# A GRU and MoE kernel on one core: the bias b_hn is added by a TensorE matmul in the exact steps, from halves made at the end of the preparation

## What is computed

```python
def cell(h, x):
    gi = x @ W_ih + b_ih
    gh = h @ W_hh + b_hh
    i_r, i_z, i_n = jnp.split(gi, 3, axis=-1)
    h_r, h_z, h_n = jnp.split(gh, 3, axis=-1)
    r = jax.nn.sigmoid(i_r + h_r)
    z = jax.nn.sigmoid(i_z + h_z)
    n = jnp.tanh(i_n + r * h_n)
    h_new = (1.0 - z) * n + z * h
```

## Time and profile before

| | us |
|---|---|
| median of three runs | 842.39 (841.79 to 842.82) |
| the profiled execution | 841.37 |
| its span in the trace | 839.6 |
| TensorE busy in the span | 803.8 (96%) |
| VectorE busy | 621.6 (74%) |
| ScalarE busy | 423.0 (50%) |
| GpSimd busy | 180.7 (22%) |

### The profile page before, as it was taken

One profiled execution on the slowest core, in us unless ns is written; L12 is line 12 of the kernel. 1 busy time (PEld: TensorE's weight loads), 2 busy tenths in 40 slices (PEclk: granted clock), 3 DMA queues, 4 the chain that ended last, 5 costly groups with the idle time before them and its releaser, 6 DMA issues.

```text
span 839.6 us, 27893 instructions
## 1 busy us (share of the span) xinstructions
PE 803.8 (96%) x11573; PEld 520.2 (62%) x11574; DVE 621.6 (74%) x2104; ACT 423.0 (50%) x885; POOL 180.7 (22%) x459
## 2 busy tenths in 40 slices
PE   7999999999999999999995799999999999999996
PEld 3446656678999899999994544454444444444442
DVE  6969999868888888888887879776667576855400
ACT  0677676645566556555544538351845184417400
POOL 1002222224333333343331020121012101210011
PEclk9999999999999999999996999999999999999998
DMA  8900000000111010000000952462246324530021
GB/s 333 368 1 3 2 2 2 2 3 7 64 54 42 17 42 5 4 4 4 5 4 14 260 182 101 151 198 53 100 150 176 73 100 150 164 86 1 1 26 26
DMA packets 24281, 62.62 MB, mean 75 GB/s; under 512 B 4384, under 2 KB 4384, under 8 KB 22304
## 3 DMA queue, kind: packets, MB, share of 16 engines
q1 hardware_dynamic: 19312, 51.42, 17.8%
q0 software_dynamic: 3584, 8.42, 5.5%
q10 hardware_dynamic: 1264, 1.08, 0.4%
HBM read 52.49 MB, written 12.62 MB: 78 GB/s over the span
## 4 chain that ended last, share of the span: by engine, by line
PE 80%; DVE 14%; ACT 2%; issue 2%; DMA 1%; POOLq 0%; DVEq 0%
PE ps L454 20%; PE ps L657 20%; PE ps L671 20%; PE ps L446 10%; DVE wa L1212 4%; PE ps L429 3%; DVE wa L1217 3%; DVE halves L1228 2%; ACT wa L767 2%; PE ps L464 2%; PE ps L419 2%; PE ps L591 1%; DVE ocand L1221 1%; PE ps L644 1%; DVE big L1504 1%
## 5 line engine op out<-in xcount | busy, mean ns | idle before, releaser
L454 PE MATMUL ps<-halves,wa 128*128 128x64 f16 x8448 | 287.7, 193 | 5.7 <-DVE halves L1228 2.2
L454 PEld LDWEIGHTS ps<-halves,wa 128*128 128x128 f16 x8448 | 271.0, 98 | 33.1 <-DVE halves L1228 14.2
L671 PE MATMUL ps<-big 128*128 128x512 f16 x768 | 166.9, 379 | 0.0
L657 PE MATMUL ps<-hx,big 128*128 128x512 f16 x768 | 166.9, 379 | 0.0
L767 ACT ACTIVATE wa<-ps,un_gates 128x128 f32<-128x128 f32 x288 | 100.2, 366 | 106.5 <-PE ps L454 100.1
L671 PEld LDWEIGHTS ps<-big 128*128 128x128 f16 x768 | 75.1, 98 | 89.9
L657 PEld LDWEIGHTS ps<-hx,big 128*128 128x128 f16 x768 | 74.9, 98 | 89.9 <-issue 0.2
L772 ACT ACTIVATE wa<-wa,un_gates 128x64 f32<-128x64 f32 x288 | 99.1, 344 | 60.0 <-DVE wa L1217 53.5
L1212 DVE SCALAR_TENSOR_TENSOR wa<-ps,bhn_s,wa 128x64 f32<-128x64 f32 x288 | 80.1, 278 | 52.9 <-ACT wa L767 52.9
L446 PE MATMUL ps<-hx,wb 128*128 128x512 f16 x432 | 106.9, 379 | 1.4 <-issue 1.4
L849 ACT ACTIVATE hx<-ps,un_hid_in 128x512 f32<-128x512 f32 x64 | 43.7, 682 | 109.2 <-PE ps L657 108.0
(11 more groups left out here) (209 smaller groups left out, 707.5 us busy)
## 6 DMA issues: line engine op xcount, KB each, us to landing
wa<-in_w SPq DMA_DIRECT2D x28, 1024.0 KB, 5.1
hs_rows<-big SPq DMA_DIRECT2D x8, 512.0 KB, 6.5
big<-in_w_hh SPq DMA_DIRECT2D x4, 768.0 KB, 19.5
wb<-in_w SPq DMA_DIRECT2D x12, 256.0 KB, 2.5
big<-in_w_ih SPq DMA_DIRECT2D x2, 1024.0 KB, 12.2
hx<-in_x_t SPq DMA_DIRECT2D x2, 1024.0 KB, 16.2
big<-in_w_ih ACTq DMA_DIRECT2D x2, 512.0 KB, 6.5
wa<-in_x_t SPq DMA_DIRECT2D x2, 512.0 KB, 6.1
```

What stands on the lines that cost most here:

```text
L454: mm = pe.matmul(gate_ps[:, j, g, :], whh_parts[:, k, w, (4 * g + j) * P:(4 * g + j + 1) * P], halves[:, src, k, h, :], start=False, stop= ...
L657: mm = pe.matmul(ps[:, m % 2, :], w1p[:, w, k, m * P:(m + 1) * P], tokT[:, t, k, :], start=(k == 0 and n == 0), stop=(k == KD - 1 and n == 2))
L671: mm = pe.matmul(ps[:, 2 + g % 2, :], hid[:, h, k, g * P:(g + 1) * P], w2p[:, w, k, :], start=(k == 0 and n == 0), stop=(k == KH - 1 and n ...
```

## The change

The vector `b_hn` comes in a second time, as a row of 512. Near the start VectorE clears the buffer `carried`, here called `bhn_row`, and ScalarE's queue loads the row into its partitions 0 and 32. At the end of the preparation the new function `split_bhn` finds a power of two as the scale, writes the scaled row in fp16 to `bhn_parts` (partition 0), what fp16 lost to partition 32, and fills `bhn_unit`, 128 x 64 in bf16, with the factor that undoes the scale. All other partitions of `bhn_parts` are zero, so one matmul of `bhn_parts` with `bhn_unit` adds the bias of a tile to all 64 columns. In each exact step `inject(j)` issues that matmul after its two. `reset` becomes a TENSOR_TENSOR in exact steps and stays as it was in rough steps.

```diff
+        bhn_row = carried[:, :, :, :].rearrange("p d k c -> p (d k c)")
+        bhn_parts = sb("bhn_parts", [P, D], F16)
+        bhn_unit = sb("bhn_unit", [P, COLS], BF16)
+        bhn_scales = sb("bhn_scales", [P, 3])
+        ROW_OF = (0, 32)
...
                     pe.matmul(gate_ps[:, j, 0:2, :], diag[:, :], gi_rz[:, c, j, part, :, cols],
                               start=(part == HIGH), stop=False, skip_group_check=True)
+                if LOW in parts:
+                    pe.matmul(gate_ps[:, j, 2, :], bhn_parts[:, j * P:(j + 1) * P], bhn_unit[:, :], start=False,
+                              stop=False, skip_group_check=True)
...
             pe.wait_ge(S["whh_ready"], WHH_PIECES)
+            pe.wait_ge(S["bhn_split"], 1)
...
             act.wait_ge(S["tables"], 1)
+            act.wait_ge(S["bhn_clear"], 1)
+            for row in ROW_OF:
+                act.dma_start(bhn_row[row:row + 1, :], b_hn).then_inc(S["bhn_loaded"], 16)
...
+            dve.memset(bhn_row, 0.0).then_inc(S["bhn_clear"], 1)
...
+            def split_bhn():
+
+                dve.wait_ge(S["bhn_loaded"], 32)
+                b_peak, b_scale, b_un = (bhn_scales[:, i:i + 1] for i in range(3))
+                link(dve.tensor_reduce(b_peak, bhn_row, AX.X, ALU.max, apply_absolute_value=True))
+                link(dve.tensor_scalar(b_peak, b_peak, 1e-30, None, ALU.max))
+                link(dve.tensor_scalar(b_un.bitcast(I32), b_peak.bitcast(I32), 0x7F800000, None, ALU.bitwise_and))
+                dve.tensor_scalar(b_scale.bitcast(I32), b_un.bitcast(I32), -1.0, float((254 + SCALE_TO) << 23),
+                                  ALU.mult, ALU.add)
+                link(dve.tensor_scalar(b_un.bitcast(I32), b_un.bitcast(I32), -float(SCALE_TO << 23), None, ALU.add))
+                link(dve.tensor_scalar(bhn_parts[:, :], bhn_row, b_scale, None, ALU.mult))
+                lows_row = slice(ROW_OF[1], ROW_OF[1] + 1)
+                dve.scalar_tensor_tensor(bhn_parts[lows_row, :], bhn_row[lows_row, :], b_scale[lows_row, :],
+                                         bhn_parts[lows_row, :], ALU.mult, ALU.subtract)
+                dve.tensor_scalar(bhn_unit[:, :], ones[:, 0:COLS], b_un, gates_scale[:, 0:1], ALU.mult,
+                                  ALU.mult).then_inc(S["bhn_split"], 1)
+
+            split_bhn()
...
-                    dve.scalar_tensor_tensor(rn[:, j, :], gate_ps[:, j, 2, :], bhn_s[:, j:j + 1], rz[:, j, 0, :],
-                                             ALU.add, ALU.mult).then_inc(S["rn_done"], 1)
+                    if bias_added:
+                        dve.tensor_tensor(rn[:, j, :], gate_ps[:, j, 2, :], rz[:, j, 0, :], ALU.mult
+                                          ).then_inc(S["rn_done"], 1)
+                    else:
+                        dve.scalar_tensor_tensor(rn[:, j, :], gate_ps[:, j, 2, :], bhn_s[:, j:j + 1], rz[:, j, 0, :],
+                                                 ALU.add, ALU.mult).then_inc(S["rn_done"], 1)
...
-                step(lambda j, c=c, cols=cols: gi[:, c, j, 2, cols], after, i % 2, KD * i, i >= ROUGH - 1, moved, ahead, between)
+                step(lambda j, c=c, cols=cols: gi[:, c, j, 2, cols], after, i % 2, KD * i, i >= ROUGH - 1, moved, ahead, between,
+                     i >= ROUGH)
```

More of the change, by code:

```diff
@@ L34, with gru_moe @@
 SEARCH_PASSES = 10
-def gru_moe(nc, x, x_t, cond_t, w_ih, w_hh, b_ih, b_hh, wg, bg, w1, w2, hs_rows, out):
+def gru_moe(nc, x, x_t, cond_t, w_ih, w_hh, b_ih, b_hh, b_hn, wg, bg, w1, w2, hs_rows, out):
     NB, T, D = x.shape
@@ L235, in gru_moe @@
             candin_ready tanh_done ocand_done start_saved check_a worst_ready worst_mm flag_ready
-            gru_over turned wg_split lg_mm lg_kept sq_done probs_in probs_stored group_made rows_copied rows_stored steps_made exp_in exp_done
+            gru_over turned bhn_clear bhn_loaded bhn_split wg_split lg_mm lg_kept sq_done probs_in probs_stored group_made rows_copied rows_stored steps_made exp_in exp_done
             above_ready chunk_peaks total_mm masks_ready sums_ready eq_mm sel_ready pos_mm pos_ready slots_ready list_mm idx_ready
@@ L1196, in w1_peak, with step @@
                 dve.tensor_reduce(peak[:, W1:W1 + 1], sq[:, :], AX.X, ALU.max).then_inc(S["w_peak"], 1)
-            def step(gi_n, after, src, base, low, moved=False, ahead=(), between=()):
+            def step(gi_n, after, src, base, low, moved=False, ahead=(), between=(), bias_added=True):
                 dst = 1 - src
@@ L1710, in laid_out @@
         'b_hh': np.asarray(inputs['L0_cond_b_hh']).reshape(-1, P).T,
+        'b_hn': np.asarray(inputs['L0_cond_b_hh'])[2 * d:].reshape(1, -1),
         'wg': np.asarray(inputs['L0_ffn_Wg']).reshape(kd, P, -1).transpose(1, 0, 2),
```

## The result

| | before | after |
|---|---|---|
| median of four runs, us | 842.41 (841.79 to 842.82) | 836.29 (835.96 to 836.93) |
| the profiled execution, us | 841.37 | 836.27 |
| its span, us | 839.6 | 834.5 |

The ratio is 0.9932 (95% interval 0.992 to 0.9945): 6.1 us faster, where 5.6 were forecast (836.7 for the median).

A forecast was written before the change was run, and what follows sets the result against it. TensorE bounds the exact steps, apart from two waits for new state tiles. 48 steps x 0.125 us = -6.0, plus 0.36 for steps 20 to 22, gives -5.6: median 836.7 us, range 835.0 to 843.0.

The forecast's parts named there:

- What bounds the step: Exact GRU steps, 5.09 us each: TensorE, its own bound except for waits of 0.22 and 0.10 us for new state tiles.
- The reset: VectorE, four per exact step: 0.22 us instead of 0.28, next start after 0.14 instead of 0.20; PSUM costs nothing extra.
- Place A: TensorE's 0.22 us wait for `blend(0)` after the injections of tiles 0 and 1; `blend(0)` was to come 0.09 us earlier.
- The matmuls: Four new per exact step, 0.030 us each: two hidden in the first wait, two on the path, +0.06 us.
- the fill matmuls: Input projection matmuls ahead of steps 20 to 22 covering the waits; there the new matmuls cost 0.12 a step, +0.36 us.
- Place B: TensorE's 0.10 us wait for `blend(1)` after tile 3's injections; was to vanish, the 126 matmuls starting 0.13 us earlier.
- rival 2: `blend(1)` stays tied to GpSimd's instructions, so Place B doesn't follow fully: 0.05 us a step, 840.4 us; chance 0.12.
- what is late next: After Place B: VectorE's `low_part(3)` reaches TensorE just before needed, also 0.15 us earlier, so it holds nothing.
- The preparation: Ahead of the first sigmoid: `split_bhn`, some 3.2 us, hidden in VectorE's 6.86 us idle; memset and DMAs covered too.
- The end: Stages behind the GRU: claimed only to start earlier as a block, with no gain of their own.
- Rival 3: The new reset on VectorE is itself held up by GpSimd: +2.3 us, 844.7; chance 0.12 together with Rival 4.
- Rival 4: New matmuls dearer, from 0.075 us each no longer covered by the waits; no own chance, counted with Rival 3 (0.12).

The follow-up runs named there:

- `e1_no_mm`: Changed kernel without the bias matmul, b_hn left out of exact steps: seven steps 34.93 us against 34.94; whole 1084.01 us, not comparable because of more correction rounds.
- `e5_low_later`: Changed kernel with the ORDER unit (LOW, 0, 3) moved behind (LOW, 2, 2), three matmuls later: 834.6 us, ratio to the kernel before 0.9917.
- `e6_all_steps`: Changed kernel with bias matmul and short reset also in the 20 rough steps, TensorE's wait ahead of step 0: 841.37 us, ratio to kernel before 1.0001.

## Why the prediction was right, point by point

- **What bounds the step** held. TensorE waited at A and B and nowhere else; with B gone and A down to 0.06, the step fell to 4.99 us.
- **The reset** takes 0.22 us, as taken from `candidate_in`, and PSUM costs nothing extra. By the Trainium skill, "VectorE: DVE Perf Modes", section "The TRN2 errata", a PSUM source costs 62 cycles more, and the reset would have stayed near 0.28 us; the 220 ns of the trace do not agree.
- **Place A** was put at 0.09 us earlier and moved by 0.08.
- **The matmuls** cost 0.03 us each and are hidden in an even step (`e1_no_mm`). Behind the fill matmuls they cost 0.12 us ahead of the first sigmoid of step 20, of 21 and of 22, the +0.36 that was worked out; from there on, in step 22 already, the gain was there.
- **Place B** vanished, by another sum than the one written. The shorter `reset(3)` was to bring `blend(1)` 0.06 us forward. It brought 0.02: the two start 0.18 us apart (304.27 and 304.45) where 0.14 were taken, since `blend` has a wait instruction of its own ahead of it in the queue, and the 0.14 was read between instructions without one. On the other hand the 0.41 us of `blend(1)`, kept as a precaution, became 0.29. Before, GpSimd's `low_part` starts 0.02 us behind it, now 0.09 (304.45 and 304.54). That this made the difference is a reading of these rows; no run tests it alone. Measured from the step's first sigmoid the 126 loads start at 2.88 us and not 3.02: 0.14 earlier, where 0.13 were worked out. So rival 2, a B that does not follow, did not happen.
- **The step of the prediction that was off** is "what is late next: `low_part(3)` ... also 0.15 us earlier, so it holds nothing". `candidate_in(3)` now starts 0.12 us behind GpSimd's `low_part` and takes 0.33 us instead of 0.21, so the chain behind it moved by 0.10 and not 0.15, and TensorE waits 0.04 for it. `e5_low_later` shows that this is the place. Hence 0.10 a step instead of 0.125: over 48 steps -4.97 in the trace instead of -6.0.
- **The preparation** was hidden. `split_bhn` took 2.9 us (3.2 estimated). Not foreseen was what its nine records on VectorE do: steps 7 and 11 +0.43 us, and among the later steps 49 and 68 became longer while 31, 40 and 59 lost more than 0.10.
- **The end.** 1.1 us were won behind the GRU, where nothing changed. From step 71 to the end the profiled executions of all these kernels but `e1_no_mm` take 397.1 to 398.8 us, without order by kernel; the two traces compared first are 1.1 apart in that. Whether it is chance is open; it makes up for most of the missing 1 us in the trace, and so the forecast of the sum, 5.6, agrees better with 5.35 and 6.1 than its parts do. That much of the agreement is luck.
- **The slower rivals.** Rival 3 is refuted by 208 resets of at most 225 ns, though they start amid GpSimd's instructions. The Trainium skill, "SBUF — State Buffer", section "SBUF: two separate sides", has VectorE contend with GpSimd where it has two SBUF inputs; the reset has one, and the trace agrees. Rival 4 is refuted by 0.029 us a matmul in `e6_all_steps`. The Trainium skill, "TensorE: Matmul & The Clock Gate", section "Back-to-back issue gap", has about 81 ns at 128 columns; the trace does not agree, with 0.029 us between starts at 64 columns and 0.055 at 128. Nor do the prediction's own terms give 844.5 for 81 ns: 0.22 us at A and 0.10 at B hold four such matmuls, and what is left is 12 x 0.081 = 0.97 in steps 20 to 22, 843.4.

## What to carry to other kernels

In a loop where engines hand tiles around, list the places where the bounding engine really starts late. An instruction added there is free up to the length of the wait (four matmuls here), the same one added in a stage where that engine is full costs its whole spacing (0.029 us each in the rough steps). The per-partition scalar on a short VectorE instruction cost 0.06 us each time here (277 ns against 220), so moving a bias into an accumulation that has waits pays, as long as what makes its operand is finished long before the first use: a wait on it in a full stage cost 4.6 us. And where two instructions' distance is taken from a row, look whether a wait stands between them in the new place.

## What the hardware showed that was not expected

- **VectorE's instruction stream stops at record numbers 128 apart.** In the trace of the changed kernel the stops of 0.14 to 0.29 us lie at VectorE's records 1471, 1727 and 1983 (256 apart, twice 128), in the kernel before at 959, 1215 and 1727 (0.18 to 0.34 us). Not every such number shows one: at 1599 and 1855 of the changed kernel VectorE is busy and goes through. Nine records more ahead of the loop slid other instructions under them; 128 more brought the old pattern back. The page of the profile counts the time as "issue". But the trace has packets of instructions near these numbers. Between 426 and 428 us of the changed kernel, around the stop at record 1983, the DMA queues carry this one packet and nothing else (8192 bytes, from 426.9 us on, 0.6 us behind the late instruction):

```profile
q14 instruction: 1, 0.01, 1.4%
```

Packets of this size and queue also start 0.9 and 0.6 us behind the late instructions of the stops at 1471 and 1727 (at 332.0 and 379.8 us), and within 1 us of records 1599 and 1855. So the stops seem to go with the loading of VectorE's instructions; no run shows that the loading is what stops it.

- **Beside GpSimd some VectorE instructions with two SBUF tiles take longer**, and the reset, which reads PSUM and one SBUF tile, never did: 0.41 instead of 0.28 us for `blend(1)` before, 0.33 instead of 0.22 for `candidate_in(3)` after, 210 to 225 ns for all resets. It hangs on when they start: `candidate_in(0)`, which in the step shown starts 0.22 us behind GpSimd's first `carry`, takes 0.23 us. The delay went from one instruction to the next when the first moved by a tenth of a us.
- **A wait of 2.09 us on TensorE** early in the kernel was followed by a stretch at half clock (0.50 from 60 to 62 us, 0.79 in the mean of 58 to 66) that the kernel without that wait does not have.
